# Softmax shift carried in the last row of the third score product, gates placed ahead of splits

## The reference

```python
xn = _layernorm(x, axis=-1)
k, q, v = xn @ Wk.T, xn @ Wq.T, xn @ Wv.T
ak = k @ Wa.T
e = jnp.einsum('biq,bjq->bij', q, ak)      # 1024 x 1024 scores per batch
alpha = jax.nn.softmax(e, axis=-1)
out = jnp.einsum('bij,bjv->biv', alpha, v @ Wb.T)
```

## Time and profile before

| what | value |
|---|---|
| median of 3 runs | 998.73 us (998.31 to 998.92) |
| the profiled execution's own time | 997.37 us |
| its span | 995.6 us |
| TensorE busy | 951.5 us (96%) |
| ScalarE busy | 742.1 us (75%) |
| VectorE busy | 551.3 us (55%) |
| GpSimd busy | 195.1 us (20%) |
| mean granted TensorE clock | 0.997 |

### The profile page before, as it was taken

The page is one execution under the profiler, slowest core; times in us unless marked ns, Lnnn a source line. Parts: engine busy times, 40 slices in busy tenths (PEclk is TensorE's granted clock), DMA queues, the critical chain, the costliest instruction groups (busy, mean ns, idle before and its releaser), DMA issues.

```text
span 995.6 us, 20044 instructions
## 1 busy us (share of the span) xinstructions
PE 951.5 (96%) x8050; PEld 538.9 (54%) x8050; DVE 551.3 (55%) x1342; ACT 742.1 (75%) x915; POOL 195.1 (20%) x142
## 2 busy tenths in 40 slices
PE   4999999999899999999989999999999999999996
PEld 3788743334388863334458884333536887433342
DVE  6645734664555664565565574456457467446544
ACT  5443699998863379999965348999895436999986
POOL 1200302331410020332340002133142003023214
PEclk9999999999999999999999999999999999999998
DMA  6000133000000023200000012310000001320000
GB/s 252 1 1 1 18 49 57 12 2 3 1 22 1 1 34 50 53 2 2 2 22 1 1 12 39 50 36 1 3 1 23 1 1 18 49 47 2 2 2 24
DMA packets 17648, 22.31 MB, mean 22 GB/s; under 512 B 2992, under 2 KB 14352, under 8 KB 17296
## 3 DMA queue, kind: packets, MB, share of 16 engines
q1 hardware_dynamic: 17552, 20.99, 10.4%
HBM read 7.85 MB, written 2.10 MB: 10 GB/s over the span
## 4 chain that ended last, share of the span: by engine, by line
PE 76%; ACT 10%; DVE 7%; issue 6%; DMA 0%; POOL 0%; DVEq 0%; ACTq 0%; POOLq 0%
PE ps L1135 76%; ACT big L1086 6%; ACT spl L1039 1%; DVE wk L571 1%; DVE mx L492 1%; DVE st L280 1%; ACT xn L1058 1%; PE ps L1155 1%; DVE wk L717 1%; DVE wk L747 0%; DMA xnext<-in_x 0%; DVE spl L468 0%; ACT qz L1034 0%; DVE flags L428 0%; ACT spl L978 0%
## 5 line engine op out<-in xcount | busy, mean ns | idle before, releaser
L1086 ACT ACTIVATE big<-ps 128x1024 f32<-128x1024 f32 x512 | 490.8, 1034 | 32.8 <-PE ps L1135 32.3
L1135 PE MATMUL ps<-big,vaug 128*32 128x512 f32 x2048 | 272.7, 604 | 2.9 <-ACT big L1086 1.6
L1135 PE MATMUL ps<-hid 32*128 32x512 f32 x1024 | 130.4, 491 | 6.1 <-ACT big L1086 4.3
L1135 PE MATMUL ps<-hid,fw_sb 128*128 128x512 f32 x416 | 101.2, 397 | 0.3 <-DVE hid L476 0.3
L1002 ACT ACTIVATE wk<-ps,cols_sb 128x512 f32<-128x512 f32 x64 | 40.5, 687 | 80.2 <-PE ps L1135 74.4
L912 POOL TENSOR_TENSOR qz<-qz,wk 128x512 f32<-128x512 f32 x32 | 41.1, 1285 | 291.0 <-DVE wk L717 291.0
L1135 PEld LDWEIGHTS ps<-hid 32*128 32x128 f32 x1024 | 49.2, 181 | 77.5 <-issue 40.8
L1135 PEld LDWEIGHTS ps<-hid,fw_sb 128*128 128x128 f32 x416 | 77.5, 188 | 18.5 <-DVE hid L476 1.1
L898 POOL TENSOR_TENSOR st<-st 128x4 f32<-128x4 f32 x16 | 16.1, 1009 | 357.4 <-DVE st L560 288.0
L1135 PEld LDWEIGHTS ps<-big,vaug 128*32 128x32 f32 x2048 | 40.9, 108 | 68.7 <-issue 35.6
L735 DVE SCALAR_TENSOR_TENSOR big<-ps,sm,big 128x128 f32<-128x128 f32 x128 | 44.4, 347 | 59.1 <-PE ps L1135 53.1
(11 more groups left out here) (221 smaller groups left out, 1567.5 us busy)
## 6 DMA issues: line engine op xcount, KB each, us to landing
hid<-spl SPq DMA_DIRECT2D x288, 32.0 KB
xnext<-in_x SPq DMA_DIRECT2D x4, 512.0 KB, 4.2
big<-in_fw SPq DMA_DIRECT2D x1, 1877.0 KB, 10.1
out<-qz SPq DMA_DIRECT2D x7, 256.0 KB, 2.3
hid<-one_row SPq DMA_DIRECT2D x16, 96.0 KB
wk<-in_lw SPq DMA_DIRECT2D x1, 1476.0 KB, 15.2
big<-in_fw SPq DMA_DIRECT2D x1, 939.0 KB, 11.9
cst_sb<-in_cst SPq DMA_DIRECT2D x1, 440.0 KB, 4.4
```

The source lines that it names most:

```text
L1086: up(ms_exp, a.activation(prob[:, at:at + 2 * CH].rearrange("p (h n) -> p h n", n=CH), ps[:, bank:bank + 2, :], ACT.Exp, scale=HDM ** -0.5))
L1135: return t_.matmul(out_, lhsT, rhs, start=start, stop=stop, **kw)
```

## The change

The shift no longer has a product of its own. The last row of the stationary side of the product with r_lo becomes ones, and the last row of r_lo becomes the negated maxima. So that nothing is lost there, the last row of the folded matrix is made zero: its last column, as it lies in PSUM, is subtracted from each column at setup (the layer norm sums to zero over the features, so the scores stay the same). The stationary side with the ones is a copy of `xt_hi`, `x_one` (`spl[:, 2]`, where the shift was), made by two DMAs of 128 rows by 512 elements and a third that writes the ones into row 127. A tile is two products (`with_high`) and the third one with `x_one` and r_lo, which takes the place of the shift product and has to wait for the row of maxima. GpSimd's zeroing goes, and so does `shift_zero`. On VectorE the gates of units 0 to 3 are placed ahead of the splits: gate 0, gate 1, split 0, gate 2, split 1, gate 3, split 2, split 3.

```diff
-        negrow, shift = spl[0:1, 2, :], spl[:, 2, :]
+        negrow, x_one = spl[P - 1:P, 1, :], spl[:, 2, :]
...
-        shift_zero = sig("shift_zero", 1, 1)
+        x_one_in = sig("x_one_in", 48)
...
+            sp.wait_ge(x_lo.sem, 2)
             sp.wait_ge(wide_ok, 1)
...
+            def key_rows(c):
+                sl = slice(c * CH, (c + 1) * CH)
+                return sp.dma_start(x_one[:, sl].bitcast(F32), xt_hi[:, sl].bitcast(F32))
+
+            def ones_in_last_row():
+                return sp.dma_start(x_one[P - 1:P, :].rearrange("p (a n) -> p a n", n=P).bitcast(F32),
+                                    one_row[0:1, :].bitcast(F32).unsqueeze(1).broadcast_to([1, S // P, P]))
+
+            for c in range(NCH):
+                up(x_one_in, key_rows(c), 16)
+            sp.wait_ge(x_one_in.sem, 32)
+            up(x_one_in, ones_in_last_row(), 16)
             for b in range(B):
...
-                sp.wait_ge(shift_zero.sem, shift_zero.at(b, 0))
                 sp.wait_ge(neg_ok.sem, neg_ok.at(b, 1))
                 up(negrow_in, sp.dma_start(negrow[:, :].bitcast(F32), negT[:, :].bitcast(F32)), 16)
...
                     up(x_in, load_x(b + 1), 16)
+                    for c in range(NCH):
+                        sp.wait_ge(x_hi.sem, x_hi.at(b, 3 + c))
+                        up(x_one_in, key_rows(c), 16)
...
                     up(stored, sp.dma_start(o[:, c * TPC:(c + 1) * TPC, :], fin[:, c * TPC:(c + 1) * TPC, :]), 16)
+                    if c == 0 and b < B - 1:
+                        sp.wait_ge(x_one_in.sem, x_one_in.at(b + 1, 32))
+                        up(x_one_in, ones_in_last_row(), 16)
...
-            done(v.tensor_copy(xn[:, 5 * D:6 * D], ps[:, 0, 0:D]), "Wa Wk")
+            done(v.tensor_copy(mrow[:, :], ps[:, 0, D - 1:D]))
+            so_far()
+            done(v.tensor_scalar(xn[:, 5 * D:6 * D], ps[:, 0, 0:D], mrow[:, 0:1], None, ALU.subtract), "Wa Wk")
...
-                for m in range(KM):
-                    gate_unit(0, m)
+                gate_unit(0, 0)
+                gate_unit(0, 1)
+                gate_split(0, 0)
+                gate_unit(0, 2)
+                gate_split(0, 1)
+                gate_unit(0, 3)
+                gate_split(0, 2)
+                gate_split(0, 3)
...
-            g_.memset(shift.bitcast(I32), 0).then_inc(shift_zero.sem, 1)
...
-                up(shift_zero, g_.memset(shift.bitcast(I32), 0))
...
-                    split3(ps[:, SC_BANKS[n_], :], *tok(jt), spl[:, 0, sl], spl[:, 1, sl], True, False)
+                    with_high(ps[:, SC_BANKS[n_], :], *tok(jt), spl[:, 0, sl])
...
+                t_.wait_ge(x_one_in.sem, x_one_in.at(b, 48))
                 t_.wait_ge(negrow_in.sem, negrow_in.at(b, 16))
...
-                    up(sc_mm, mm(ps[:, SC_BANKS[n_], :], one_row[:, :], shift[:, h * CH:(h + 1) * CH], False, True))
+                    up(sc_mm, mm(ps[:, SC_BANKS[n_], :], x_one[:, jt * P:(jt + 1) * P], spl[:, 1, h * CH:(h + 1) * CH], False, True))
```

More of the change, by code:

```diff
@@ L485, in gate_unit, with gate_split @@
                     up(gated, v.scalar_tensor_tensor(h_, ps[:, L1_BANKS[c][m % 2] + 1, :], col("w2s", m), h_, ALU.mult, ALU.mult))
+                def gate_split(c, m):
+                    n_ = c * KM + m
                     v.wait_ge(gated.sem, gated.at(b, n_ + 1))
@@ L551, in _ @@
                     gate_unit(1, m)
+                    gate_split(1, m)
                 act_units(0, 8, 1)
@@ L1308, in _ @@
                         score_products(n_)
-                    h = n_ // NT
+                    h, jt = n_ // NT, n_ % NT
                     if b == 0 and n_ == 13:
```

## The result

The changed kernel takes 984.73 us (median of 4 runs, 983.64 to 985.63) where the kernel before takes 998.52 in the same comparison (997.46 to 998.92). The ratio is 0.9866, with a 95% interval of 0.9853 to 0.9880: 13.8 us are gained, where 13.1 were forecast, and the predicted 985.6 is 0.9 us above the measured time. Further on, two executions far above all others of their kernels are left out, one of 1452.73 us and one of 1741.21.

What follows compares the result with a forecast made beforehand. TensorE was taken to bound the kernel, busy 96% of the span. About 3.28 us per batch, 13.1 in all, off the median of 998.73 gave 985.6 us, with a range of 983.0 to 989.0.

Steps and rivals of the forecast that it cites:

- The price of a product: In the score tiles, each removed matmul is worth 0.233 us, the distance between starts; 64 of them are 14.9 us.
- Two of 16 products buy nothing: Products dropped from tiles 0 and 1 gain nothing, as the transposition stays at 281.79; 14 left, 3.26 us per batch.
- rival B: All 16 products per batch count, ahead of the transposition too: gain 14 to 14.9 us, 983.8 to 984.7; chance 0.07.
- Gates ahead of splits: VectorE's new order has all four gates ready before TensorE asks, and the held 0.08 us is gained.
- The row's transfer: The row of maxima lands 2.3 us behind its issue, so the first x_one product waits 0.05 us.
- ScalarE as a new limit: The exponentials that tile 12 waits for end at 291.11, before TensorE reaches it at 291.28: nothing lost, by 0.2 us.
- rival A: Consumers set the pace: silu 3 stays, tile 12 waits 0.33 us; gain 10.6 to 11.8, 987 to 988; chance 0.10.
- The key side and the setup: Key-side copies land before their need, and VectorE's 0.3 us more at setup ends in idle time: cost nothing.
- The sum: Per batch 0.48 us to the first new product plus 2.80 over 12 tiles, 3.28; in all 13.1 us.

Runs made afterwards that it cites:

- the run with the copies in series: The changed kernel with each key-side copy made four times, each after the landing of the one before: 996.76 us, beside 984.18 for the changed kernel.

## Why the prediction was right, point by point

**The price of a product.** 0.233 us, from the distance of the starts and not from the 396 ns of the grouped view. It held in the main: one more product per tile costs 3.01 us per period, where 14 at 0.233 would be 3.26. It was a little high for the new kernel, where the 24 products of tiles 4 to 11 run 0.227 us apart. At 0.227, 14 are 3.18, and the added product does away with two small losses of the new kernel, 0.12 us ahead of the transposition and 0.06 at tile 12. The Trainium skill's 131 ns for a 512-column matmul in a stream ("TensorE: Matmul & The Clock Gate", back-to-back issue gap) would have made it 1.8 us per period for 14 products; the measured 3.01 decides against it for these operands.

**Two of 16 products buy nothing.** Nearly right. The transposition stays bound to the last maximum and TensorE idles ahead of it. But it moved up by 0.12 us against the maximum (1.40 to 1.28), which I had ruled out. Before, it was TensorE that held the transposition: it started 0.23 us behind the last product, which is the full pace (281.56 and 281.79), and without those products it can start 1.28 behind the maximum's start. That is the small part of rival B that came true.

**Gates ahead of splits.** Gate 2 starts at 282.10 and so ends at 282.84, a microsecond ahead of tile 4 (283.86); gate 3 ends at 284.56, ahead of tile 6 at 285.2. With the old order both places wait, and the experiment puts that at 0.87 us per batch. The mis-sized term is gate 0: I had it 0.07 us ahead of its need, and `l1_unit(0, 2)` starts 0.33 us behind its predecessor and its second matmul 0.35 behind the first. Some 0.2 us per batch went there. That is more than the whole of 3.10 against 2.96, since the 0.05 of waiting for the row fell away. The gates follow VectorE's last maximum just as the transposition does: `l1_unit(0, 2)` starts 1.95 us behind the maximum's start, close to the 1.98 of the forecast, so what the earlier transposition gained was lost again at gate 0.

**The row's transfer.** The mechanism was right (it hides) and the size off: 1.93 us from issue to use, where I took 2.3 from a store of 256 KB. The 0.05 us of waiting does not exist and the slack is 0.57. The Trainium skill's 2.0 us ("DMA: Bandwidth & Descriptors", the section on the anatomy of one DMA), which the page gives for GpSimd's path, was the better estimate for this transfer of the SP queue. The 1.93 measured agrees with it.

**ScalarE as a new limit.** I had 0.2 us to spare at tile 12. There is none; the changed kernel's batch 2:

```profile
525.84 0.39 PE L1163 MATMUL ps<-spl 128*128 128x512 f32 x1
526.02 0.19 PEld L1163 LDWEIGHTS ps<-spl,xt_hi 128*128 128x128 f32 x1 [0.22 <-ACT big L1044]
526.06 0.46 PE L1163 MATMUL ps<-spl,xt_hi 128*128 128x512 f32 x1
526.35 0.40 PE L1163 MATMUL ps<-spl,xt_lo 128*128 128x512 f32 x1
```

The weight load waits for the exponential and the tile loses 0.06 us (0.29 between two starts). The margin went from two sides: the first exponential starts 4.84 us behind the transposition in batch 1 (284.69), where the forecast had 4.67, because unit 3 came later, and tile 12 was reached as early as forecast because the tiles before it were quicker (0.68 us each, not 0.70). So rival A's place was right and its price was not.

**The key side and the setup.** Both cost nothing that a trace shows, as forecast; whether they make the slow start likelier is open. In the changed kernel the copies go out at 260.1, the row of ones at 274.7, and the x_one products never wait. The longer work on VectorE at setup ends in an idle stretch (1.49 us before, 1.23 after).

**The sum.** Against the profiled execution 13.1 us were forecast. Two executions in which the full pace comes at the same point of the setup, 995.6 and 982.2, differ by 13.4: 0.2 ahead of the first transposition, then 3.18, 3.42, 3.37 and 3.20. The errors of up to 0.2 us per batch went both ways: the transposition and the quicker tiles gave 0.12 and 0.14 more than forecast, the stretch between them 0.14 less. That they cancel in part is luck. So is the place of the median: the forecast's own band began at 984.7, where rival B's ended, and the changed kernel's three medians, 984.18, 984.73 and 985.13, lie on both sides of it.

## What to carry to other kernels

Price a removed instruction by the distance between starts in a full stream of the stage, and count only those copies that stand behind the last wait of another engine. Then ask what the removed work was covering: here the order of VectorE's gates was worth some 0.1 us per batch before and 0.87 after, and it had to be changed together with the products. When a stage shrinks, work out the next limit's distance too: a second product of the same price brought a third of the first.

## What the runs showed of the hardware

Early in the span TensorE runs matmuls of 512 columns 0.42 us apart or 0.23 us apart, and when it changes differs between executions of one program: within the four row-score matmuls that start at 29.57 in one (1.81 us for the four, where 2.29 are all at the slower pace) and only at 36.8 in the other. That is the 1.25 us of the span. Ahead of the late change TensorE had been busy from 24 to 31 us and 2.67 of the next 3 us. The distances differ by a factor of 1.8. In the run with the copies in series the slower one, 0.43 us, goes with a granted clock of 0.50 (53 to 54 us), so the two belong to TensorE's levels of 1.2 and 2.4 GHz. But the granted clock doesn't always tell it. In the execution that changes at 36.8 it reads 1.00 throughout (window, PE busy, PEld, DVE, ACT, POOL, PEclk, DMA share, GB/s):

```profile
31.00:34.00 3.00, 2.67 (x5) 1.23 (x6) 2.98 (x4) 0.00 (x0) 0.65 (x1) 1.00 0.30 115
34.00:36.00 2.00, 2.00 (x7) 1.61 (x7) 1.90 (x2) 0.00 (x0) 0.00 (x0) 1.00 0.00 0
```

The full pace can also be lost again without a long wait. In the run with the copies in series the matmuls from 32.13 to 34.8 us run at the full pace, and from there to 38.1 they are 0.42 us apart; here the granted clock does fall, to 0.72 from 34 to 36. TensorE had been busy for 2.04 of the 3 us before 34, much as in the second execution of the kernel before (2.06), which kept its pace. The medians of two comparisons of one kernel differ by up to 1 us here (984.2 and 985.1), and these changes of pace may be a part of it; that was not separated.

The distance of 0.233 us in the kernel before and 0.227 in tiles 4 to 11 of the changed one is not explained. It is not the number of products, since four products per tile ran 0.227 apart as well.
